# A unit triangle kept under a mask, and the whole of M copied from a product, in a delta-rule kernel

## The reference

```
xn = layernorm(x)
# s: delta-rule attention, 4 heads, k and q of 128, v of 64
k = k * rsqrt(sum(k*k) + 1e-12);  q = q * 128**-0.5;  beta = sigmoid(xn @ Wb)
S = S + k (beta * (v - k^T S))^T ;  o = q^T S          # token by token
s = (o * rsqrt(mean(o*o) + eps) * norm_w * silu(g)) @ Wo
# f: 8 experts, each token takes the one with the largest logit
f = square(relu(xn @ fc[e])) @ proj[e]
out = x + s * silu(f)
```

## Time and profile before

| | us |
|---|---|
| median of 3 runs (lowest to highest) | 783.77 (781.04 to 786.33) |
| the profiled execution | 784.05 |
| its span, from first to last instruction | 782.3 |
| TensorE busy | 722.2 |
| VectorE busy | 542.5 |
| GpSimd busy | 396.9 |
| ScalarE busy | 354.2 |
| mean granted clock of TensorE | 0.994 |

### The profile page before, as it was taken

One profiled execution on the slowest core, in us unless ns is written; L12 is line 12 of the kernel. 1 busy time (PEld: TensorE's weight loads), 2 busy tenths in 40 slices (PEclk: granted clock), 3 DMA queues, 4 the chain that ended last, 5 costly groups with the idle time before them and its releaser, 6 DMA issues.

```text
span 782.3 us, 23109 instructions
## 1 busy us (share of the span) xinstructions
PE 722.2 (92%) x9442; PEld 621.6 (79%) x9442; DVE 542.5 (69%) x1169; ACT 354.2 (45%) x768; POOL 396.9 (51%) x411
## 2 busy tenths in 40 slices
PE   5666899999999999999999999999999999999976
PEld 4555798878889788887888878888888887979853
DVE  4779457566575665756556577877777777787788
ACT  5551354445444454444445344444444453545432
POOL 3571538354473545626454354647464646545351
PEclk9998999999999999999999999999999999999999
DMA  9420973452335434343354333333333323323076
GB/s 300 145 83 1 386 287 143 153 213 116 130 129 197 162 115 176 134 177 130 116 204 152 131 130 116 128 115 126 116 129 116 129 116 129 131 108 103 22 232 220
DMA packets 37753, 116.33 MB, mean 149 GB/s; under 512 B 3664, under 2 KB 24400, under 8 KB 27664
## 3 DMA queue, kind: packets, MB, share of 16 engines
q1 hardware_dynamic: 33904, 104.62, 36.7%
q0 software_dynamic: 3744, 10.23, 3.9%
HBM read 101.33 MB, written 13.50 MB: 147 GB/s over the span
## 4 chain that ended last, share of the span: by engine, by line
PE 68%; DVE 13%; POOL 7%; issue 6%; DMA 3%; ACT 2%; SPq 0%; DVEq 0%; POOLq 0%
PE bank L509 17%; PE bank L520 16%; PE bank L589 4%; PE bank L483 4%; PE bank L485 3%; PE bank L484 3%; PE bank L555 3%; PE bank L629 2%; PE bank L647 2%; PE bank L638 2%; PE bank L731 2%; PE bank L539 2%; POOL XTl L2446 2%; PE bank L568 2%; DVE M L1768 2%
## 5 line engine op out<-in xcount | busy, mean ns | idle before, releaser
L520 PE MATMUL bank<-wts,hT 128*128 128x256 f32 x624 | 170.9, 393 | 0.0
L509 PE MATMUL bank<-xsT,wts 128*128 128x128 f32 x1248 | 166.0, 281 | 1.2 <-DMA wts<-in_pj 1.1
L509 PEld LDWEIGHTS bank<-xsT,wts 128*128 128x128 f32 x1248 | 150.6, 192 | 4.7 <-DMA wts<-in_pj 1.2
L1785 DVE TENSOR_TENSOR Pm<-bank,lvl_mask 128x256 f16<-128x256 f32 x180 | 68.1, 417 | 62.6 <-PE bank L629 61.9
L520 PEld LDWEIGHTS bank<-wts,hT 128*128 128x128 f32 x624 | 105.4, 191 | 7.3
L2446 POOL TENSOR_TENSOR XTl<-f_t,XTh 128x512 f16<-128x512 f32 x32 | 40.0, 1257 | 125.6 <-DVE XTh L1723 125.4
L1215 ACT CAST Z<-bank 128x256 f16<-128x256 f32 x180 | 59.3, 376 | 96.7 <-PE bank L647 96.6
L1796 DVE TENSOR_TENSOR M<-bank,M 128x256 f16<-128x256 f32 x180 | 68.8, 418 | 38.7 <-PE bank L638 37.8
L1160 ACT ACTIVATE hT<-bank 128x512 f32<-128x512 f32 x78 | 46.7, 599 | 46.9 <-PE bank L509 46.9
L2466 POOL TENSOR_TENSOR ImM<-ident,M 128x512 f32<-128x512 f16 x30 | 35.1, 1189 | 42.1 <-DVE M L1796 42.1
L555 PE MATMUL bank<-xT,wq 128*128 128x128 f16 x768 | 49.3, 222 | 4.1 <-DVE qT16l L1728 3.6
(11 more groups left out here) (257 smaller groups left out, 1975.5 us busy)
## 6 DMA issues: line engine op xcount, KB each, us to landing
wts<-in_fc SPq DMA_DIRECT2D x39, 1024.0 KB, 4.9
wts<-in_pj SPq DMA_DIRECT2D x39, 1024.0 KB, 8.4
wts<-in_x SPq DMA_DIRECT2D x10, 512.0 KB, 8.2
wts<-y_d SPq DMA_DIRECT2D x4, 1024.0 KB, 9.6
out_x<-wts SPq DMA_DIRECT2D x16, 256.0 KB, 2.8
xn_d<-wts SPq DMA_DIRECT2D x3, 1024.0 KB, 4.4
x_first<-in_x SPq DMA_DIRECT2D x4, 512.0 KB, 16.4
wts<-in_x SPq DMA_DIRECT2D x4, 256.0 KB, 3.5
```

Of the source, the lines that this page charges most:

```text
L509: ins = pe.matmul(psum[bank[n]][:, (c % 4) * P:(c % 4 + 1) * P], fcw[r][:, k, c * P:(c + 1) * P], xsT[:, k, :], start=(k == 0), stop=(k == ...
L520: ins = pe.matmul(psum[bank[0]][:, 0:D], hT[:, c, :], pjw[r][:, c, :], start=(c == 0), stop=(c == HC - 1))
L1785: dve.tensor_tensor(h4(Pms[last(m)], b).rearrange("p h (n c) -> p h n c", c=s), half4(level_bank(m, b)).rearrange("p h (n c) -> p h n c", ...
```

## The change

It does three things. The strict triangle is no longer made by a product with a mask of -1 into f32_t: a buffer `unit` gets the identity once from GpSimd, and X32 copies the bank into it where the mask `up_strict` is not zero, so that `unit` holds a unit triangle; its sign is that of the product, and the signs of the masks `pair` and `lvl_mask` and of Fr turn with it. M is no longer preset with the identity on VectorE: M0 multiplies Z with all 128 columns of the identity, and M0c evicts the whole. Because `unit` and the identity give what ImM gave, GpSimd's ImM and VectorE's wait for it go. And every list of calls of TensorE, ScalarE, VectorE and GpSimd is written out in a new order.

```diff
-                            ins = pe.matmul(half4(level_bank(m, b))[:, h, :], Zs[last(m)][:, H * b + h, :],
-                                            evens(ident16[:].unsqueeze(1), 1)[:, 0].rearrange("p n c -> p (n c)"),
+                            ins = pe.matmul(bank4(level_bank(m, b))[:, h, :], Zs[last(m)][:, H * b + h, :], ident16[:],
                                             start=True, stop=True)
...
-                    act.copy(evens(h4(Ms[last(m)], b), 1), half4(level_bank(m, b)).unsqueeze(3)).then_inc(M0_ok[b], 1)
+                    act.copy(h4(Ms[last(m)], b), bank4(level_bank(m, b))).then_inc(M0_ok[b], 1)
...
-                    fr.on(Gp[b], kl_ok[b], kh_ok[b])
-                    dve.tensor_tensor(h4(f32_t, b), bank4(KG_BANK[b]), up_neg[:].unsqueeze(1).to_broadcast([P, H, P]),
-                                      ALU.mult).then_inc(X32_ok[b], 1)
+                        dve.wait_ge(unit_ok, 1)
+                    fr.on(Gp[b])
+                    fr.on(Xl_ok[b], Xh_ok[b], back=1)
+                    dve.copy_predicated(h4(unit, b), up_strict[:].bitcast(I32).unsqueeze(1).to_broadcast([P, H, P]),
+                                        bank4(KG_BANK[b])).then_inc(X32_ok[b], 1)
...
-                    dve.tensor_copy(h4(XT[0][a % 2], b), h4(f32_t, b)).then_inc(Xh_ok[b], 1)
+                    dve.tensor_copy(h4(XT[0][a % 2], b), h4(unit, b)).then_inc(Xh_ok[b], 1)
...
-                    fr.on(PTp[b], Xl_ok[b], Xh_ok[b])
+                    fr.on(PTp[b], kl_ok[b], kh_ok[b])
                     dve.tensor_tensor(h4(f32_t, b), bank4(KG_BANK[b]),
...
-                    dve.tensor_copy(h4(Ms[last(m)], b), ident16[:].unsqueeze(1).to_broadcast([P, H, P]))
...
-                    lv.on(Fp[b], ImM_ok[b])
-                    dve.tensor_tensor(h4(Fr[m % 2], b), bank4(level_bank(m, b)), h4(ImM, b), ALU.add).then_inc(F_ok[b], 1)
+                    lv.on(Fp[b])
+                    dve.tensor_tensor(h4(Fr[m % 2], b), ident[:].unsqueeze(1).to_broadcast([P, H, P]),
+                                      bank4(level_bank(m, b)), ALU.subtract).then_inc(F_ok[b], 1)
...
+                def unit_diagonal():
+                    pool.tensor_copy(unit[:], ident[:].unsqueeze(1).to_broadcast([P, NS, P])).then_inc(unit_ok, 1)
...
-                def ImM_(m, b):
-                    lv = At(pool, m)
-                    stage_of(pool, m, NL - 1, b, dM_ok, last_dM_ok)
-                    lv.on(F_ok[b], back=1)
-                    pool.tensor_tensor(h4(ImM, b), ident16[:].unsqueeze(1).to_broadcast([P, H, P]), h4(Ms[last(m)], b),
-                                       ALU.subtract).then_inc(ImM_ok[b], 1)
```

## The result

The changed kernel takes 778.49 us (median of 9 runs, 776.55 to 781.38) against 783.37 (9 runs, 781.04 to 786.33): the ratio is 0.993, 95% interval 0.9914 to 0.9947. That is 0.7% less: clear of the noise, inside the 1% that the prediction counts as the same, and 3.5 us under its 782. The profiled execution took 778.46 us, with a span of 776.7.

What follows compares the result with a forecast made beforehand. TensorE, busy 722.2 of 782.3 us, was taken as the bound, so only its waits count. 784 - 10 (ramp) + 7 (three-tile steps) + 2.5 (two-tile steps) - 1.5 (tail) = 782 us; range 764 to 795.

Steps and rivals of the forecast that it cites:

- the collision: Three-tile steps: GpSimd's run of gates, X_l and P_l meets VectorE's MZ; M0 stalls 2.0 to 2.5 us, not 1.49.
- Ramp, -10: Before the first expert: reordered routing brings tile_e, tokens and first expert earlier; gain 5 to 12 us, taken as 10.
- the forecast span: Ramp: the first expert starts at 78 to 82 us in place of 87.33.
- Three-tile step, +1.0: Each of seven three-tile steps: longer M0 stall, 0.23 for its columns, about 0.2 elsewhere; +1.0 us, between -1.1 and +1.6.
- the signs on record: Three-tile steps: period 48.2 to 49.3 us, M0 waiting over 2, Z copies or pair products at 1 or more beside X_l or P_l.
- the sum by that rule: Three-tile steps: VectorE gets in after one GpSimd operation, a step costs about half as much more; total near 778 us.
- Two-tile step, +0.5: Each of five two-tile steps: M0's stall about 1.1 us, waits at F give back some 0.5; +0.5, between -0.7 and +1.4.
- Tail, -1.5: After 745 us: copies of M and ImM go from the last chunks; -1.5 us, between -4 and +2.
- C: X32 on VectorE takes two passes, hidden in three-tile steps but on the path of two-tile ones; total 788 us, chance 0.08.
- B: All twelve steps: GpSimd's run also holds R_h and R_l, so U starts late; total 794 us, chance 0.16.
- D: The ramp does not move: the first expert waits for something else, its tokens, as late as before; total 790, chance 0.12.
- A: Steps: the new GpSimd run does not meet MZ; steps fall by 1.1 and 0.7 us, total 761, chance 0.22.

Runs made afterwards that it cites:

- the late experts: The changed kernel with tile_e made behind VectorE's second product with pos_l, near 69 us in place of 57: 778.86 us, against 778.49.
- X_l ahead of the gates: The changed kernel with X_l, X_l, P_l of a three-tile step moved ahead of its last two gates on GpSimd: 771.17 us, ratio 0.9844 to the kernel before.

## Why the prediction was right, and where its sizes were off

**Right in the result, and in the mechanism with its sizes too large.** The forecast was no change that can be told, by a gain in the ramp that the steps hand back in part. That is what the table shows, and two experiments show it by their parts: the old ramp puts the time back to 783.63, and moving GpSimd's run out of the way of the doubling takes 7.3 us off. But the collision in the three-tile step keeps M0's wait of before and does not lengthen it; what the step hands back beyond the old period is smaller than forecast, and from other terms.

**Ramp, -10, measured -7.8 in the profile and -3.9 to -5.1 between medians.** The first expert came in the forecast span (80.71), and it is the tokens that hold it. But choose and tile_e came earlier than I walked them, and the early tile_e gave nothing: the late experts show that. Beyond the tokens the chain of chunk 0 holds TensorE at nearly the same time, so the first expert alone was never worth as much as it moved. How much of the ramp's difference comes from the edits themselves isn't settled: with the old ramp lists the first ru stood at 115.95 in one profile, of the fastest of four executions, and at 119.46 in another, of one of the slowest of ten.

**Three-tile step, +1.0, measured +0.40 (+0.54 with the first and the last).** Three addends: M0's columns 0.23, others 0.2, and M0's stall, 2.0 to 2.5 for 1.49. The first two make up the measured 0.40 by themselves, if not as I split them: M0's eight products, up to the start of the next one, take 0.34 us before and 0.46 in the edits in the old order, 0.12 more, so that 0.3 fell elsewhere. The stall is the term that was too large, for it did not grow: the rows give 0.70 and 0.60 for 1.49. I had let VectorE wait for the end of the whole GpSimd run and Zo end 2 us behind it. Instead VectorE was let in after single operations, a Z copy at 307.57, a Pm behind P_l and a Zo behind X_l, so that at the end of the run (310.19) only the end of the first Zo and the three short operations of the second half were left, and the last Zo ended 1.3 us behind it. By the signs on record the collision thus came in part: Pm and Zo took over 1 us beside P_l and X_l, but the period of 48.08 lies below the 48.2 that I named, and M0 does not wait over 2 us. The Trainium skill, page "SBUF — State Buffer", section "Who interferes with whom", has the shared ports go, in VectorE's two-port modes, to whoever issues first, for one whole instruction; the sum by that rule was 778. In the three-tile step Pm and Zo, two-input products of which the sentence does not speak, fit it: one GpSimd operation for each, 1.38 and 1.28 us. In the two-tile step the Z copy does not: its 1.52 us end 0.18 behind the second P_l. What decides between the two no run here shows. That 778 is nearly the measured time is no proof of the rule either, since the ramp was off too, the other way.

**A reading that was wrong.** I put M0's eviction at nothing because dM uses it first. It is L of the first level that reads M first. With the change the weight load of that L waits 0.18 us for it, at 313.10; in the new ramp with the old steps the same wait came to 2.65.

**Two-tile step, +0.5, measured +0.03 to +0.1.** M0's stall grew, from 0.31 to 0.69 us by the rows and not to 1.1, and the wait at F (0.28 us for Z before) is gone. The edits are worth more here than I gave them: 0.53 us a step in the old order.

**Tail, -1.5, measured -1.7.** As forecast.

**What the sum didn't hold apart.** I priced edits and order together, stage by stage. Apart, they are of opposite sign: the edits gain some 5 to 6 us in the old order, the new ramp some 4 to 6, and the new lists of the steps lose 4 to 6. The nearness of the sum to the measurement is in part luck: its errors are of opposite sign, 2 to 6 us too much gain in the ramp and 5.6 too much loss in the steps.

**The rivals.** C is out (0.72 us). B did not occur in the change: R_l took 1.13 in places, but U was not late; with X_l ahead of the gates a part of it came, 0.43 us. D, that the ramp does not move, is out in its result, but its reason, that early experts without early tokens are worth nothing, is what the late experts showed. D's own sum was off: without the ramp's 10 us the forecast gives 792, not 790. So was the span of 774 to 790 for the forecast: half the bounds on ramp and steps give about 770 to 789. A did not come by the change itself; with X_l ahead of the gates its three-tile step came (47.0 us for 46.6), but the whole was 771.17, ten above A's 761.

## What to carry to other kernels

An operation that leaves a side engine is worth what the operations beside it stop waiting for: look at which GpSimd operation runs at the moment when VectorE's critical few begin, and move that one into a stretch where GpSimd is idle, here 7 us were free just ahead, and look again at what it meets there (R_l, in this case). When a change brings edits and a new order together, run the edits in the old order first: here they alone gave the whole gain, and the best kernel takes the old two-tile lists, and the new ramp and three-tile lists with a GpSimd run moved in each. And a first event that comes earlier, like the first expert, is worth only the distance to what is late next.

## What was not expected of the hardware

TensorE's granted clock in the ramp differs between executions of nearly the same ramp, and moves it by as much as parts of the change do. The stretch of the first 20 expert products with its row, in the edits in the old order and then in the old ramp with new steps:

```profile
84.09:86.40 2.31, 2.31 (x21) 2.30 (x22) 1.79 (x5) 1.37 (x4) 0.00 (x0) 1.00 1.01 417
...
84.09 2.47 PE L510 MATMUL bank<-xsT,wts 128*128 128x128 f32 x20 [0.32 <-ACT xsT L1169]
```

```profile
85.95:89.91 3.96, 3.96 (x21) 3.95 (x21) 1.94 (x5) 1.46 (x4) 1.34 (x2) 0.57 1.01 419
...
85.95 4.13 PE L510 MATMUL bank<-xsT,wts 128*128 128x128 f32 x20 [0.46 <-DMA wts<-in_pj]
```

The same 20 products take 2.47 us at 1.00 and 4.13 at 0.57, mostly the level of 1.2 GHz. Just ahead of the slow stretch TensorE had waited 1.53 us for a gather and 0.46 for the weights, ahead of the fast one 1.04 and 0.32. Over the whole span the mean granted clock was between 0.980 and 0.996 in these profiles; from 20 us to the first ru it was 0.97 in the kernel before, 0.93 in the change, 0.98 in the edits in the old order and 0.90 with the old ramp. A difference in the ramp of 2 or 3 us between two profiles is thus no verdict on two kernels, and the medians were used. The ramp's -7.8 stands under the same doubt: the change was profiled at the lower clock of the two.
